# Eleven tables by matmul instead of ten, one-hots of two tables in one comparison, and row buffers for a whole chunk

## The reference

```python
e = jnp.stack([tbl_0[ids[:, 0]], tbl_1[ids[:, 1]], ...], axis=1)      # [2048, 27, 128]
z = einsum('bnd,bmd->bnm', e, e)[:, c, r]                             # the 351 pairs below the diagonal
h = jnp.concatenate([z.reshape(2048, -1), dense_ctx], axis=1)         # [2048, 367]
h = jnp.maximum(h @ W_top1 + b_top1, 0.0)                             # 512 wide
h = jnp.maximum(h @ W_top2 + b_top2, 0.0)                             # 256 wide
y = h @ W_top3
```

## Time and profile before

| | |
|---|---|
| Median of 3 runs | 390.16 us (388.52 to 391.35) |
| The profiled execution | 389.1 us |
| Its span, first to last instruction | 387.3 us |
| Mean granted TensorE clock | 0.96 |
| PE, PEld (weight loads), DVE, ACT, POOL busy | 87%, 79%, 59%, 50%, 68% |
| DMA traffic | 45.73 MB, mean 118 GB/s |

### The profile page before, as it was taken

The page is one execution under the profiler, slowest core; times in us unless marked ns, Lnnn a source line. Parts: engine busy times, 40 slices in busy tenths (PEclk is TensorE's granted clock), DMA queues, the critical chain, the costliest instruction groups (busy, mean ns, idle before and its releaser), DMA issues.

```text
span 387.3 us, 15244 instructions
## 1 busy us (share of the span) xinstructions
PE 337.4 (87%) x6096; PEld 304.2 (79%) x6096; DVE 226.7 (59%) x689; ACT 195.1 (50%) x318; POOL 262.9 (68%) x279
## 2 busy tenths in 40 slices
PE   0767699979979999979999997979989996986777
PEld 0656599779969898869989896969988996965765
DVE  4799998548743586438862785438862884411010
ACT  2457446535644465455554664436645554536223
POOL 5777747777777777777777777777777777772000
PEclk9899999989989999999999998999999998996889
DMA  6999542853364326533275328432474327433210
GB/s 180 240 242 258 163 112 54 195 113 105 94 168 105 102 60 164 120 95 95 70 187 121 95 54 203 93 99 76 108 165 102 97 60 195 94 84 80 41 37 0
DMA packets 68596, 45.73 MB, mean 118 GB/s; under 512 B 53478, under 2 KB 56934, under 8 KB 68535
## 3 DMA queue, kind: packets, MB, share of 16 engines
q1 hardware_dynamic: 58237, 26.65, 28.9%
q0 software_dynamic: 8704, 17.84, 18.3%
q10 hardware_dynamic: 1594, 0.31, 0.4%
HBM read 39.02 MB, written 5.76 MB: 116 GB/s over the span
## 4 chain that ended last, share of the span: by engine, by line
PE 62%; DMA 13%; issue 9%; POOL 7%; DVE 4%; ACT 3%; SPq 2%; ACTq 1%; POOLq 0%
PE lookup_ps L508 31%; PE gram_ps L527 10%; PE layer_ps L544 7%; PE gather_ps L493 7%; POOL rows L463 7%; DMA rows<-tbl,index 6%; DMA emb<-tbl 6%; PE layer_ps L556 5%; DVE one_hot L753 2%; PE layer_ps L564 2%; DVE table_lo L760 1%; DMA gram_dram<-gram 1%; ACT emb L620 1%; SPq L344 1%; SPq L389 1%
## 5 line engine op out<-in xcount | busy, mean ns | idle before, releaser
L463 POOL DMA_INDIRECT rows<-tbl,index x272 | 262.1, 964 | 88.5 <-issue 74.8
L753 DVE TENSOR_SCALAR one_hot<-ids_all,row_number 125x256 fp32r<-125x256 int32 x648 | 202.9, 378 | 101.6 <-PE lookup_ps L508 99.1
L508 PE MATMUL lookup_ps<-one_hot,table_hi 125*128 125x256 f32 x640 | 177.9, 310 | 21.9 <-DVE one_hot L753 17.8
L508 PE MATMUL lookup_ps<-one_hot,table_lo 125*128 125x256 f32 x640 | 163.0, 286 | 0.5 <-issue 0.5
L508 PEld LDWEIGHTS lookup_ps<-one_hot,table_hi 125*128 125x128 f32 x640 | 124.6, 195 | 30.7 <-issue 24.1
L508 PEld LDWEIGHTS lookup_ps<-one_hot,table_lo 125*128 125x128 f32 x640 | 125.1, 195 | 0.9 <-issue 0.7
L620 ACT ACTIVATE emb<-gather_ps 128x384 f32<-128x384 f32 (+1 forms) x80 | 86.4, 1080 | 37.7 <-PE gather_ps L493 37.0
L626 ACT ACTIVATE emb<-lookup_ps 128x256 f32<-128x256 f32 x80 | 56.1, 701 | 31.9 <-PE lookup_ps L508 31.8
L527 PE MATMUL gram_ps<-emb 128*26 128x27 f32 x4096 | 59.0, 195 | 11.3 <-issue 8.3
L527 PEld LDWEIGHTS gram_ps<-emb 128*26 128x26 f32 x4096 | 47.9, 107 | 24.3 <-issue 14.1
L493 PE MATMUL gather_ps<-identity,rows 128*128 128x128 f32 x272 | 46.6, 290 | 11.0 <-DMA rows<-tbl,index 10.0
(11 more groups left out here) (36 smaller groups left out, 104.8 us busy)
## 6 DMA issues: line engine op xcount, KB each, us to landing
ids_all<-lookup_ids SPq DMA_DIRECT2D x44, 256.0 KB, 3.4
gram_dram<-gram SPq DMA_DIRECT2D x62, 87.8 KB
emb<-tbl SPq DMA_DIRECT2D x10, 448.0 KB
rows<-tbl,index POOLq DMA_INDIRECT x272
z<-gram_dram SPq DMA_DIRECT2D x14, 117.0 KB
z<-gram_dram SPq DMA_DIRECT2D x7, 91.0 KB
emb<-w SPq DMA_DIRECT2D x3, 192.0 KB
emb<-tbl SPq DMA_DIRECT2D x10, 52.0 KB
```

The costliest lines, as they stand in the source:

```text
L463: pool.indirect_dma_start(rows[g][:, j * DIM:(j + 1) * DIM], None, tables[f], bass.IndirectOffsetOnAxis(index[p][:, h, f:f + 1], 0)).then_ ...
L508: last = nc.tensor.matmul(lookup_ps[k % LOOKUP_BANKS], table[:, k, row, :], one_hot[u % UNIT_RING][:, r, :], start=(row == 0 and table is ...
L753: last = nc.vector.tensor_scalar(one_hot[u % UNIT_RING][:, r, :], table_ids, row_number[0:LOOKUP_PARTS, row:row + 1], None, ALU.is_equal)
```

## The change

Four things change together.

1. `N_LOOKUP` goes from 10 to 11: one more table of 1,000 rows is done by matmul, and 16 features are gathered. Slots are 4 of 4 features per half, 8 per chunk.
2. There is a row buffer and a semaphore for each of the 8 slots of a chunk (`ROWS_FREE = N_GATHERS`), so a buffer is reused a whole chunk later.
3. A unit is now one row number of two tables (a "part" of two tables): one comparison of 125 x 512 and four matmuls into the two halves of one PSUM bank, of which only the very first matmul has the start flag. Parts 0 to 4 have 8 units each; part 5 is the eleventh table alone, with 4 units of two row numbers and two comparisons each. That is 44 units a chunk; `EARLY_UNITS` goes to 28. ACT copies a part (512 columns) at once. Ids come in 6 loads instead of 5, each when the units of its part are made.
4. In both copies to `emb` the order of elements is now sample outside, feature inside, so the writes go in runs of 4 (gathers) or 2 (lookups) neighbouring elements and the reads of PSUM have a step; before, each write stood 27 elements from the next.

In the start, ACT makes `table_hi` of tables 2p+2 and 2p+3 at the units with row 2 and row 6 of part p (`TABLES_AT`), DVE makes their `table_lo` right after its units with row 3 and row 7 (`LOWS_AT`), DVE makes `table_lo` of tables 0 and 1 before the first unit, and the low part of W1 after part 0. With 44 units, `first_order` puts slot G0 after unit 5, G1 after unit 13, G2 after unit 20 and G3 after unit 28.

The diff, cut to its core:

```diff
-N_LOOKUP = 10
+N_LOOKUP = 11
 LOOKUP_ROWS = min(TABLE_ROWS)
 LOOKUP = [f for f in range(FEATURES) if TABLE_ROWS[f] == LOOKUP_ROWS][:N_LOOKUP]
...
 K_ROWS = tuple(PAIR_ROWS + d for d in DENSE_ROWS)
-SLOT_SIZES = (4, 4, 3, 3, 3)
+SLOT_SIZES = (4, 4, 4, 4)
 SLOTS = [list(range(sum(SLOT_SIZES[:g]), sum(SLOT_SIZES[:g + 1]))) for g in range(len(SLOT_SIZES))]
 N_GATHERS = HALVES * len(SLOTS)
...
 GRAM_BANKS = 2
-UNIT_ROWS = 2
-UNITS_PER_TABLE = PART_ROWS // UNIT_ROWS
-N_UNITS = N_LOOKUP * UNITS_PER_TABLE
+PAIR = 2
+N_PARTS = -(-N_LOOKUP // PAIR)
+PART_TABLES = [list(range(N_LOOKUP))[part * PAIR:(part + 1) * PAIR] for part in range(N_PARTS)]
+UNITS = [(part, row) for part in range(N_PARTS) for row in range(0, PART_ROWS, PAIR // len(PART_TABLES[part]))]
+N_UNITS = len(UNITS)
+UNITS_TO = [sum(part <= n for part, _ in UNITS) for n in range(N_PARTS)]
 UNIT_RING = 4
-ID_PARTS = 5
-TABLES_PER_PART = N_LOOKUP // ID_PARTS
-UNITS_PER_PART = N_UNITS // ID_PARTS
 LATE_PART = 4
...
 STAGES = 4
 TABLES_AHEAD = 2
-EARLY_UNITS = 24
+TABLES_AT, LOWS_AT = (2, 6), (3, 7)
+EARLY_UNITS = 28
 GRAMS_FROM, GRAMS_TO = 0.08, (0.64, 0.94)
...
         identity = sbuf("identity", [P, P])
         index = [sbuf(f"index{p}", [P, HALVES, FEATURES], i32) for p in range(2)]
...
         row_number = sbuf("row_number", [P, PART_ROWS])
-        ids_all = [sbuf(f"ids_all{part}", [P, TABLES_PER_PART, CHUNK], i32) for part in range(ID_PARTS)]
-        one_hot = [sbuf(f"one_hot{i}", [LOOKUP_PARTS, UNIT_ROWS, CHUNK], fp32r) for i in range(UNIT_RING)]
+        ids_all = [sbuf(f"ids_all{part}", [P, len(PART_TABLES[part]), CHUNK], i32) for part in range(N_PARTS)]
+        one_hot = [sbuf(f"one_hot{i}", [LOOKUP_PARTS, PAIR, CHUNK], fp32r) for i in range(UNIT_RING)]
...
         final = tower(spare[:, 0:K_TILES, :], spare[:, K_TILES:o1_tiles, :], spare[:, o1_tiles, :])
         gather_ps = [psum(f"gather_ps{i}") for i in range(GATHER_BANKS)]
-        lookup_ps = [psum(f"lookup_ps{i}")[:, 0:CHUNK] for i in range(LOOKUP_BANKS)]
+        lookup_ps = [psum(f"lookup_ps{i}") for i in range(LOOKUP_BANKS)]
         gram_ps = [psum(f"gram_ps{i}") for i in range(GRAM_BANKS)]
...
-        ROWS_FREE = len(SLOTS)
+        ROWS_FREE = N_GATHERS
         GATHER_FREE = GATHER_BANKS
         LOOKUP_FREE = LOOKUP_BANKS
...
                 sp.dma_start(index[p][:, :, :].rearrange("p h f -> p (h f)"), ids[bass.ds(c * P, P), :]).then_inc(index_ready[p], 16)
             def load_ids(c, part):
-                src = lookup_ids[bass.ds(c, 1), part, :].rearrange("c b -> (c b)")
+                columns = slice(PART_TABLES[part][0] * CHUNK, (PART_TABLES[part][-1] + 1) * CHUNK)
+                src = lookup_ids[bass.ds(c, 1), columns].rearrange("c b -> (c b)")
                 sp.dma_start(ids_all[part][:, :, :].rearrange("p k b -> p (k b)"), src.partition_broadcast(P)
                              ).then_inc(ids_ready[part], 16)
...
                 sp.wait_ge(table_hi_ready, k - STAGES + 1)
                 sp.wait_ge(table_lo_ready, k - STAGES + 1)
                 load_table(k)
-                if k - 1 < ID_PARTS:
+                if k - 1 < N_PARTS:
                     load_ids(0, k - 1)
-            for part in range(ID_PARTS):
+            for part in range(N_PARTS):
                 prefetch_ids(1, part)
...
                     for j, n in enumerate(SLOTS[g]):
                         f = ORDER[n]
                         pool.indirect_dma_start(
-                            rows[g][:, j * DIM:(j + 1) * DIM], None, tables[f],
-                            bass.IndirectOffsetOnAxis(index[p][:, h, f:f + 1], 0)).then_inc(rows_in[g], 16)
+                            rows[k][:, j * DIM:(j + 1) * DIM], None, tables[f],
+                            bass.IndirectOffsetOnAxis(index[p][:, h, f:f + 1], 0)).then_inc(rows_in[k], 16)
             nc.gpsimd.iota(row_number_int[:, :], [[1, PART_ROWS]], base=0, channel_multiplier=PART_ROWS
...
                 g = k % len(SLOTS)
-                pe.wait_ge(rows_in[g], (c * HALVES + k // len(SLOTS) + 1) * 16 * len(SLOTS[g]))
+                pe.wait_ge(rows_in[k], (c + 1) * 16 * len(SLOTS[g]))
                 pe.wait_ge(gather_out, c * N_GATHERS + k + 1)
                 for j in range(len(SLOTS[g])):
                     last = nc.tensor.transpose(gather_ps[k % GATHER_BANKS][:, j * P:(j + 1) * P],
-                                               rows[g][:, j * DIM:(j + 1) * DIM], identity[:, :])
+                                               rows[k][:, j * DIM:(j + 1) * DIM], identity[:, :])
                 last.then_inc(transposed, 1)
             def lookup_unit(c, u):
-                k, part = divmod(u, UNITS_PER_TABLE)
-                if part == 0:
-                    pe.wait_ge(lookup_out, c * N_LOOKUP + k + 1)
+                part, row = UNITS[u]
+                out, tables_of = lookup_ps[part % LOOKUP_BANKS], PART_TABLES[part]
+                if row == 0:
+                    pe.wait_ge(lookup_out, c * N_PARTS + part + 1)
                 pe.wait_ge(unit_ready, c * N_UNITS + u + 1)
-                for r in range(UNIT_ROWS):
-                    row = part * UNIT_ROWS + r
+                for j in range(PAIR):
+                    n, r = (j, row) if len(tables_of) == PAIR else (0, row + j)
                     for table in (table_hi, table_lo):
-                        last = nc.tensor.matmul(lookup_ps[k % LOOKUP_BANKS], table[:, k, row, :],
-                                                one_hot[u % UNIT_RING][:, r, :],
-                                                start=(row == 0 and table is table_hi),
-                                                stop=(row == PART_ROWS - 1 and table is table_lo))
+                        last = nc.tensor.matmul(out[:, n * CHUNK:(n + 1) * CHUNK], table[:, tables_of[n], r, :],
+                                                one_hot[u % UNIT_RING][:, j, :],
+                                                start=(r == 0 and n == 0 and table is table_hi),
+                                                stop=(r == PART_ROWS - 1 and table is table_lo), skip_group_check=True)
                 last.then_inc(unit_free, 1)
...
                 if what == "gather":
                     gather(c, k)
                 else:
-                    if c == 0 and k % UNITS_PER_TABLE == 0:
-                        pe.wait_ge(table_hi_ready, k // UNITS_PER_TABLE + 1)
-                        pe.wait_ge(table_lo_ready, k // UNITS_PER_TABLE + 1)
+                    part, row = UNITS[k]
+                    if row == 0:
+                        pe.wait_ge(table_hi_ready, PART_TABLES[part][-1] + 1)
+                        pe.wait_ge(table_lo_ready, PART_TABLES[part][-1] + 1)
                     lookup_unit(c, k)
...
                 n0, n = SLOTS[g][0], len(SLOTS[g])
                 act.wait_ge(transposed, c * N_GATHERS + k + 1 + ROWS_FREE)
-                dst = emb[p][:, h * P // PER_TILE:(h + 1) * P // PER_TILE, n0:n0 + n, :].rearrange("d t f s -> d f t s")
-                src = gather_ps[k % GATHER_BANKS][:, 0:n * P].rearrange("d (f t s) -> d f t s", f=n, s=PER_TILE)
+                dst = emb[p][:, h * P // PER_TILE:(h + 1) * P // PER_TILE, n0:n0 + n, :]
+                src = gather_ps[k % GATHER_BANKS][:, 0:n * P].rearrange("d (f t s) -> d t f s", f=n, s=PER_TILE)
                 nc.scalar.activation(dst, src, ACT.Copy).then_inc(gather_out, 1)
-            def copy_lookup(c, p, k):
-                act.wait_ge(unit_free, c * N_UNITS + (k + 1) * UNITS_PER_TABLE + UNIT_RING)
-                src = lookup_ps[k % LOOKUP_BANKS].rearrange("d (t s) -> d t s", s=PER_TILE)
-                nc.scalar.activation(emb[p][:, :, len(GATHER) + k, :], src, ACT.Copy).then_inc(lookup_out, 1)
+            def copy_lookup(c, p, part):
+                act.wait_ge(unit_free, c * N_UNITS + UNITS_TO[part] + UNIT_RING)
+                n0, n = len(GATHER) + PART_TABLES[part][0], len(PART_TABLES[part])
+                dst = emb[p][:, :, n0:n0 + n, :]
+                src = lookup_ps[part % LOOKUP_BANKS][:, 0:n * CHUNK].rearrange("d (f t s) -> d t f s", f=n, s=PER_TILE)
+                nc.scalar.activation(dst, src, ACT.Copy).then_inc(lookup_out, 1)
...
                 last = nc.scalar.activation(w1_hi[0:K_ROWS[k], k, :], w1_sb[0:K_ROWS[k], k, :], ACT.Copy)
             last.then_inc(w1_hi_ready, 1)
             for what, c, k in first_order():
-                table, part = divmod(k, UNITS_PER_TABLE)
                 if what == "gather":
                     copy_gather(c, c, k)
-                elif part == UNITS_PER_TABLE - 1:
-                    if table + TABLES_AHEAD < N_LOOKUP:
-                        table_high(table + TABLES_AHEAD)
-                    copy_lookup(c, c, table)
+                    continue
+                part, row = UNITS[k]
+                if row in TABLES_AT and (part + 1) * PAIR + TABLES_AT.index(row) < N_LOOKUP:
+                    table_high((part + 1) * PAIR + TABLES_AT.index(row))
```

(31 more changed lines are left out.)

18 lines of the change are left out of this document (9 added, 9 removed).

## The result

The changed kernel takes 399.94 us (median of 396.14, 398.75, 401.14 and 401.74); the kernel before, run beside it, 389.89 (388.52 to 391.35). The ratio is **1.0262, 95% interval 1.0211 to 1.0313**: slower, and within 2.3 us of the forecast 397.7. The profiled execution is the fastest of the four, 396.14 us with a span of 394.3; it stands 7.0 us above the profiled one of before.

A forecast was written before the change was run, and what follows sets the result against it. POOL was taken to set the loop's pace by a little, with PE close behind and bounding after the change, DVE bounding the start; 389.1 + 9.9 + 1.7 - 2 - 1 = 397.7 us, own range 392 to 403.

The forecast's parts named there:

- The start: Chunk 0, before chunk 1: a table-preparation chain across DVE, PE and ACT delays it by +9.9 us, with bounds +7.1 to +15.8.
- The four stalls: DVE in chunk 0, parts 0 to 3: idle until ACT's rounding of an odd table (`table_hi`), 8.1 us in all.
- The first rival: Chunk 0: ACT rounds tables 3, 5, 7, 9 before DVE's last unit of the part, no stalls; 389.6 us, chance 17%.
- Chunk 1: PE's chunk before the loop: no waits for rows to give back, so the added table's work costs +1.7 us.
- The loop: Three turns of two chunks, each 85.8 us against 86.5: -2 us, from -5 to 0.
- the late stage: PE's stage with the other 16 units and the layers: keeps its units, taken as 22.8 us, near 22.7 in the trace.
- the cadence: POOL's pace in the gathers: 1.25 us apiece, so 32 x 1.25 = 40.0 us a chunk.
- POOL falls below PE: With 16 gathers fewer, POOL needs 40.0 us a chunk, may run a chunk ahead, and PE's waits for rows go.
- The second rival: Gathers: POOL was the only bound, so 16 fewer take 20 us off, giving 369 us; chance 6%.
- The tail: After the last gathers: rows are there early, but ACT's copies still stand before the grams; -1 us, from -3 to 0.
- The third rival: DVE's 512-element comparison is dear, 0.65 us a unit, copies 1.24; loop gives nothing: 405.6 us, chance 15%.
- signs of being wrong: Forecast wrong if chunk 1 starts before 54 us, or a turn takes under 84 or over 88.

## Why the prediction was right or wrong

**The start: right in kind and place, 8.4 us for 9.9.** The four stalls are where they were put and ended by the release that was named; 2.90, 2.52, 1.71 and 2.61 us, 9.7 in all for the forecast 8.1. DVE's own work came out shorter: a unit 0.397 us from start to start (18.69, four in 1.67 with the last one's length in it) for 0.475, and the copy 0.68 for 0.90. Both lay near the low end of my bounds. By what the Trainium skill (VectorE: DVE Perf Modes, perf-mode tier table) says of such an operation I had estimated the unit near 0.41. By its 16-byte lines (SBUF — State Buffer, Door 1: the DMA port swizzle) I had estimated the copy at 0.65. With both the start would have been +7.2. The measured durations agree with these estimates; no run separates the pages' reasons from others. Rounding earlier shows the cause: 5.8 of the 8.4 us go with one pair of numbers.

**The first rival (the start hides the chain) is false** for this order: it decided once copy, transposes and rounding fit behind the slot, and they did not, even with the short copy. With the rounding ahead of the copy, two of the four stalls are gone and two are 1.06 and 0.87 us.

**Chunk 1: +1.7 forecast, -2.3 measured. The step that failed is leaving what its late stage had lost** (18.89 us). I named that loss and then took it to return. It did not: pauses fell from 3.3 to 1.4 us, and the stretch at 1.2 GHz, worth 1.7 us at most (18.89 x 0.09), went; together 3.6 of the 4.1 us. Nor was the loss an accident of one execution. The same stage took 18.89, 17.81 and 18.37 us in the three traces with ten tables (before, buffers alone, buffers and copy), each with 2.5 to 3.3 us of pauses and a granted clock of 0.90 to 0.91, and 14.12 to 15.91 us in the six with eleven tables on the chips where PE ran normally, with 0.6 to 1.7 us of pauses and a clock of 1.00 in all but one (0.89, in the execution of 407.59 us). It goes with the order of ten tables; why, stays open. The early stage grew by 1.8 us (17.14 to 18.93), as forecast.

**The loop: -2 forecast, -0.3 measured.** Early stages were forecast at 19.1 and are 18.6 to 19.0. The failed term is the late stage, taken as 22.8 from the cleanest of before. Six late ones and the turns were 6 x 22.8 + 6 = 142.8 us and took 146.8; six early ones were 114.6 and took 112.7. The stage shown has no turn and loses 1.73 us in pauses of PE's instructions. The waits for rows did go, 7.5 us of them in the loop. But pauses that no wait explains went from 3.5 to 6.4 us there, and waits for ACT from 2.0 to 3.2.

**POOL: the cadence was wrong.** 1.25 us was carried over without asking what the new comparison does to its neighbour. At 1.35 it is 32 x 1.35 = 43.2 us a chunk, not 40.0, and the last gather starts at 347.9, hardly before the 351.30 of the earlier trace rows. (The 13.7 us of waits for PE were read wrong as well: but for one of 3.99 us they are the pauses of 0.30 us that stand between any two gathers.) "POOL falls below PE" held only by a hair, since PE's chunk takes 43.3. The time did not suffer: with shorter gathers POOL ended 14 us sooner and PE gained nothing. The second rival (369 us) fell by this twice over: PE bounds at once, and POOL's saving was gone, for 256 gathers of 80 ns more are 20 us, as much as 16 gathers fewer were to save.

**The tail: -1 forecast, +1.2 measured.** PE's pauses before gram matmuls, 2.78 us the longest, came to 7.5 us for 4.8, more than the rows' being early gave.

**The third rival (long comparison dear) is false**: 0.397 us, and DVE waits 88.4 us for PE.

**The sum was helped by luck.** The four terms are off by -1.5, -4.0, +1.7 and +2.2 us, which leaves -1.6 in the profiled execution (396.1 for 397.7), and the median lies 3.8 us above that execution. None of the signs of being wrong came: chunk 1 starts after 54 us, and a turn takes 259.5 / 3 = 86.5.

Against the median: rounding earlier takes the ratio from 1.0233 to 1.0116. From there to the eleventh table done the old way (1.0040) are another 3.0 us by spans (393.2 and 390.2), although its start is 1.8 us the longer. They lie in the tail (44.8 and 41.5 us, first gram to the end), the loop (262.2 and 261.0) and chunk 1 (0.3). **Open** is why. The buffers are not it (1.0032 with them), and shorter comparisons did not help. Kernels with the new order of the gather copy show 12.9 to 18.1 us of pauses before grams, those with the old one 7.2 to 8.3, and in the one pair with ten tables that differs by this order alone the traces say the same (13.7 and 7.7 us, loops of 258.5 and 254.1). But the medians of that pair do not differ (0.9853 and 0.9866), and its two traces are of the slowest execution of the one (388.09, the others 384.57 to 384.86) and the fastest of the other. That the copy's order brings the pauses is thus not shown. The other rival, the pairing of tables in units and banks, was not tested by itself on a chip where PE ran normally.

## What to carry to other kernels

Before work is put into an engine's fixed order, look at what stands in front of it there: a copy that waits for a third engine made every preparation behind it late, and moving two numbers gave back half of the loss (5.0 of 9.4 us on one chip). Where two engines are within some per cent of each other, moving work from one to the other gains nothing, while taking away what makes the bounding one wait (here, a buffer for each slot, 1.3%) does. A stage that was clean once is a lower limit and no forecast, and one that lost time once may lose it for a reason that the change takes away: the same stage in the traces of other kernels tells which.
